# Attention and 4-bit feed-forward on one core: t for pairs of batches with its halves through DRAM, and the feed-forward as seven block products

## The reference

```python
x = x + attended(layernorm(x), ctx)      # x, ctx: (8, 256, 1024) float32
x = x + layernorm(x) @ weights + bias    # weights 1024 x 1024
# attended(text, features):
Q = text @ Wq.T + bq;  K = features @ Wk.T + bk
attn = softmax(Q @ K.T / sqrt(1024));  attended = attn @ features
# weights, from 4-bit codes of qweight, qzeros and a group index of the rows:
weights = scales[g_idx] * (where(code > 0, 1, -1) - zeros[g_idx])
```

## Time and profile before

| | |
|---|---|
| median of 3 runs (lowest, highest) | 623.54 us (623.06, 624.27) |
| the profiled execution: span | 620.2 us |
| busy: TensorE, weight loads, VectorE | 601.2, 555.8, 385.9 us |
| busy: ScalarE, GpSimd | 143.5, 125.4 us |
| matmuls | 3938 |
| moved by DMA | 60.25 MB |

### The profile page before, as it was taken

One profiled execution on the slowest core, in us unless ns is written; L12 is line 12 of the kernel. 1 busy time (PEld: TensorE's weight loads), 2 busy tenths in 40 slices (PEclk: granted clock), 3 DMA queues, 4 the chain that ended last, 5 costly groups with the idle time before them and its releaser, 6 DMA issues.

```text
span 620.2 us, 10380 instructions
## 1 busy us (share of the span) xinstructions
PE 601.2 (97%) x3938; PEld 555.8 (90%) x3938; DVE 385.9 (62%) x647; ACT 143.5 (23%) x278; POOL 125.4 (20%) x100
## 2 busy tenths in 40 slices
PE   5999999999999999999999999979999999999997
PEld 4999999999999999999999999967788888888886
DVE  5764564874865647657476674596766566567551
ACT  5321121242231322314224142154100100100100
POOL 3450000011030210301103012066132132122130
PEclk9999999999999999999999999998999999999999
DMA  8812400005042150421603306014411321221201
GB/s 275 246 35 68 165 6 2 1 1 204 2 182 89 67 204 0 161 110 46 225 0 142 129 26 246 1 35 175 166 68 70 116 85 68 106 97 68 101 35 68
DMA packets 23796, 60.25 MB, mean 97 GB/s; under 512 B 1704, under 2 KB 9904, under 8 KB 23776
## 3 DMA queue, kind: packets, MB, share of 16 engines
q1 hardware_dynamic: 23776, 59.98, 26.5%
HBM read 43.20 MB, written 16.78 MB: 97 GB/s over the span
## 4 chain that ended last, share of the span: by engine, by line
PE 90%; DVE 3%; issue 2%; DMA 2%; POOL 2%; ACT 1%; SPq 0%; ACTq 0%; POOLq 0%
PE bank L911 27%; PE bank L913 27%; PE bank L912 27%; PE bank L1005 2%; PE bank L978 2%; PE bank L1088 2%; DMA xin<-in_L_xattn_Wk 2%; POOL shared L395 1%; DVE shared L578 1%; PE bank L926 1%; DVE wrow L787 1%; PE bank L927 1%; ACT shared L433 0%; PE bank L1013 0%; ACT proj_hi L433 0%
## 5 line engine op out<-in xcount | busy, mean ns | idle before, releaser
L578 DVE TENSOR_TENSOR shared<-bank,shared 128x512 fp32r<-128x512 f32 x96 | 64.6, 687 | 139.3 <-ACT shared L433 139.3
L911 PE MATMUL bank<-shared,proj_hi 128*128 128x256 f32 x512 | 150.6, 294 | 0.0
L913 PE MATMUL bank<-shared,proj_lo 128*128 128x256 f32 x512 | 144.8, 283 | 0.0
L912 PE MATMUL bank<-shared,proj_hi 128*128 128x256 f32 x512 | 144.7, 283 | 0.0
L433 ACT ACTIVATE shared<-bank 128x512 fp32r<-128x512 f32 x96 | 56.0, 602 | 326.1 <-PE bank L1088 160.2
L911 PE MATMUL bank<-proj_hi,shared 128*128 128x512 f32 x256 | 101.7, 397 | 1.0 <-DVE proj_lo L578 1.0
L912 PE MATMUL bank<-proj_lo,shared 128*128 128x512 f32 x256 | 100.4, 392 | 0.0
L913 PE MATMUL bank<-proj_hi,shared 128*128 128x512 f32 x256 | 100.3, 392 | 0.0
L911 PEld LDWEIGHTS bank<-shared,proj_hi 128*128 128x128 f32 x512 | 98.0, 191 | 1.9
L912 PEld LDWEIGHTS bank<-shared,proj_hi 128*128 128x128 f32 x512 | 98.2, 192 | 0.4
L913 PEld LDWEIGHTS bank<-shared,proj_lo 128*128 128x128 f32 x512 | 98.0, 191 | 0.0
(11 more groups left out here) (112 smaller groups left out, 818.9 us busy)
## 6 DMA issues: line engine op xcount, KB each, us to landing
cin<-in_ctx SPq DMA_DIRECT2D x8, 1024.0 KB, 4.7
xres<-in_x SPq DMA_DIRECT2D x8, 1024.0 KB, 6.5
x_scratch<-xres SPq DMA_DIRECT2D x8, 1024.0 KB, 3.9
xin<-in_x SPq DMA_DIRECT2D x7, 1024.0 KB, 4.7
xin<-x_scratch SPq DMA_DIRECT2D x8, 512.0 KB, 3.2
cin<-x_scratch SPq DMA_DIRECT2D x8, 512.0 KB, 3.3
out<-xin SPq DMA_DIRECT2D x8, 512.0 KB, 2.6
xres<-in_L_xattn_Wq SPq DMA_DIRECT2D x7, 512.0 KB, 3.8
```

Source lines behind the costliest of these rows:

```text
L578: return dve.tensor_tensor(out_, full, hi.bitcast(F32), ALU.subtract).then_inc(done, 1)
L911: pe.matmul(out_, a_hi, b_hi, start=start, stop=False, skip_group_check=True)
L912: pe.matmul(out_, a_hi, b_lo, start=False, stop=False, skip_group_check=True)
L913: return pe.matmul(out_, a_lo, b_hi, start=False, stop=stop, skip_group_check=True)
```

## The change

**t by pairs.** The loop over batches is split in two. First all t: for four pairs of batches p, eight blocks j, 24 matmuls of 512 columns (two batches side by side) into banks 0 to 3 in turn. ScalarE and VectorE write both halves of a block into one of four staging buffers, and SyncE stores them to DRAM (256 KB each, pieces of 1 KB). The x of the next pair, its LayerNorm, `row_terms` for two batches, `pick` and `weights` (two eighths in a pair, at j = 1 and j = 4; gathers on TensorE) stand between the blocks. A finished eighth of the weights goes to DRAM too.

**Attention.** Then eight batches: scores(b) with `c_tr(b+1)` and `p_tr(b-1)` in it, then pv(b-1). tT is one buffer in four chunks; SyncE loads chunk c of t(b+1) when scores(b) has used it. Contexts have three buffers, xres two; the buffer of cn (context rows in halves) is single. In between, SyncE loads the weights (`load_w`, row tiles k and k + 4, 1 MB in one buffer); VectorE makes four sums of their quarters (`right_sums`), ScalarE and GpSimd the halves of seven blocks (`right_hi`, `right_lo`).

**Feed-forward.** For each batch, y (256 x 1024) is a 2 x 2 block matrix and so are the weights. Four sums s1 to s4 of y's blocks and four t1 to t4 of the weights' give seven products in Winograd's form (a11 b11, a12 b21, s2 t2, s1 t1, s3 t3, s4 b22, a22 t4), each 4 slices x three matmuls of 512 columns, in banks that partly go on accumulating from product to product; `added` adds each bank into the residual. a21 is copied by ScalarE, low halves of the sums are GpSimd's, of the plain blocks VectorE's. y is normalised without a stride (`ln_apply`). All loops are unrolled.

```diff
+LEFT = ("a11", "a12", "s2", "s1", "s3", "s4", "a22")
+RIGHT = ("b11", "b21", "t2", "t1", "t3", "b22", "t4")
...
+        t_stage_hi = [at(f"t_stage_hi{i}", 146.25 + 4 * i, [P, 2 * S], F32R) for i in range(4)]
...
+        cT_hi = at("cT_hi", 66, [P, NB, S], F32R)
+        cT_lo = at("cT_lo", 74, [P, NB, S], F32R)
+        tT_hi = at("tT_hi", 98.0625, [P, NB, S], F32R)
+        tT_lo = at("tT_lo", 106.0625, [P, NB, S], F32R)
+        cn_hi = at("cn_hi", 130.25, [P, QT, D], F32R)
+        cn_lo = at("cn_lo", 138.25, [P, QT, D], F32R)
...
+        w_stage = at("w_stage", 146.25, [P, 2, D], F32)
...
+        PICK = {(p, 1 + 3 * i): 2 * p + i for p in range(PAIRS) for i in range(2)}
...
+            def load_xres(b):
+                if b >= 2:
+                    sp.wait_ge(s_x1st[b % 2], 16 * (b // 2))
+                else:
+                    sp.wait_ge(s_w, 2 * NB)
+                    for n in range(2):
+                        sp.wait_ge(s_wst[n], 16 * 4)
...
+            def load_w(k):
+                if k == 0:
+                    for n in range(2):
+                        sp.wait_ge(s_ts[n], 32 * 8)
+                        sp.wait_ge(s_wst[n], 16 * 4)
+                else:
+                    sp.wait_ge(s_rlo, N_PROD * k)
+                for i in range(2):
+                    sp.dma_start(w_stage[:, i, :], w_by_tile[k + KH * i]).then_inc(s_wsl, 16)
...
+                    for dram, stage, made in ((th_dram, t_stage_hi, s_thi), (tl_dram, t_stage_lo, s_tlo)):
+                        sp.wait_ge(made, n + 1)
+                        sp.dma_start(dram[bs, :, j, :].rearrange("b p q -> p b q"),
+                                     stage[n % 4].bitcast(F32).rearrange("p (b q) -> p b q", b=2)
+                                     ).then_inc(s_ts[n % 4], 16)
...
+            load_xres(0)
+            load_xres(1)
+            load_ctx(2)
+            load_w(0)
+            for b in range(B):
+                if b + 1 < B:
+                    for c in range(3):
+                        load_t(b + 1, c)
+                if b + 2 < B and b > 0:
+                    load_ctx(b + 2)
+                if b + 1 < B:
+                    load_t(b + 1, 3)
+                if b == B - 2:
+                    sp.wait_ge(s_x1st[0], 16)
+                    sp.dma_start(yin, x1_dram[0]).then_inc(s_yl, 16)
+                if b > 0:
+                    store_x1(b - 1)
+                    if b + 1 < B:
+                        load_xres(b + 1)
+                if b in (2, 4, 6):
+                    load_w(b // 2)
...
+            made = list(R_HI)
+            for b in range(B - 1):
                 ctx_lo(b)
+                if b == B - 2:
+                    rsqrt(B)
+                if b in SPLIT:
+                    right_lo(SPLIT[b], made[:3])
+                elif b - 1 in SPLIT:
+                    right_lo(SPLIT[b - 1], made[3:])
+            right_lo(KH - 1, made[:1])
             ctx_lo(B - 1)
...
+            for name in L_LO_P:
+                left_lo(0, name)
+            add_bias(0)
+            rsqrt(B + 1)
+            for b in range(B):
+                if b + 1 < B:
+                    add_bias(b + 1)
+                    for name in L_LO_P:
+                        left_lo(b + 1, name)
+                    if b + 2 < B:
...
+            def ctx_hi(b):
+                act.wait_ge(s_cl[b % 3], 16 * (b // 3 + 1))
+                if b:
+                    act.wait_ge(s_pv, 4 * b)
+                for kt in range(QT):
+                    copy(cn_hi[:, kt, :], cin[b % 3][:, kt, :]).then_inc(s_cnhi, 1)
...
+            row_terms(0)
+            row_terms(1)
...
+            def right_sums(k):
+                dve.wait_ge(s_wsl, 32 * (k + 1))
+                (b11, b12), (b21, b22) = ([w_stage[:, i, h * HALF:(h + 1) * HALF] for h in range(2)] for i in range(2))
+                r = r_sum[k]
+                dve.tensor_tensor(r["t1"], b12, b11, ALU.subtract).then_inc(s_rsum, 1)
...
                 softmax_bias(b)
+                if b > 0:
+                    for g in range(4):
+                        residual(b - 1, g)
+                if b in SPLIT:
+                    right_sums(SPLIT[b])
+                if b == B - 2:
+                    y_stats(0)
+                    ln_apply(yin, B, s_yn)
...
+            def added(b, n):
+                dve.wait_ge(s_ff, N_PROD * b + n + 1)
+                t, h = ((0, 0), (0, 0), (0, 1), (1, 1), (1, 1), (0, 1), (1, 0))[n]
+                if n == 0:
+                    dve.wait_ge(s_rb, QT * (b + 1))
+                if n in (1, 4, 5):
+                    dve.wait_ge(s_acc, N_PROD * b + {1: 1, 4: 4, 5: 3}[n])
+                part = res[b % 3][:, t, h * HALF:(h + 1) * HALF]
+                dve.tensor_tensor(part, part, prod_bank(b, n)[:, :], ALU.add).then_inc(s_acc, 1)
...
+            for b in range(B):
+                left_lo(b, "a22")
+                if b + 1 < B:
+                    y_stats(b + 1)
+                    if b == 0:
+                        for g in range(4):
+                            residual(B - 1, g)
+                    added(b, 0)
+                    ln_apply(yin, B + b + 1, s_yn)
+                else:
+                    added(b, 0)
+                added(b, 1)
+                added(b, 2)
+                added(b, 3)
+                if b + 1 < B:
+                    left_sum(b + 1, "s1")
+                    left_sum(b + 1, "s2")
+                    left_lo(b + 1, "a11")
+                added(b, 4)
+                if b + 1 < B:
+                    left_sum(b + 1, "s3")
+                    left_lo(b + 1, "a12")
+                added(b, 5)
+                if b + 1 < B:
+                    left_sum(b + 1, "s4")
...
-            def scores(b, last=False):
-                pe.wait_ge(s_clo, NU * (b + 1))
-                s_w.wait(pe, 2 * b + 2)
...
+                        ins = three(bank[n % 4][:, :], m_hi[:, i, js], m_lo[:, i, js],
+                                    xT_hi[p % 2][:, i, :], xT_lo[p % 2][:, i, :], i == 0, i == NB - 1)
...
+            def y_tr(b, names):
+                for name in names:
+                    t, d = int(name[1]) - 1, int(name[2]) - 1
+                    pe.wait_ge(s_yn, QT * (b + 1))
...
+            def scores(b):
+                wait(pe, s_e, QT * (b - 1))
+                for j in range(NB):
+                    if j % 2 == 0:
+                        pe.wait_ge(s_clo, 4 * b + j // 2 + 1)
+                        pe.wait_ge(s_tl[j // 2], 32 * (b + 1))
+                    if b < 2 and j == 0:
+                        pe.wait_ge(s_tlo, NB * PAIRS)
                     for q in range(QT):
                         qs = slice(q * P, (q + 1) * P)
+                        ins = three(bank[b % 2][:, q * S:(q + 1) * S], tT_hi[:, j, qs], tT_lo[:, j, qs],
                                     cT_hi[:, j, :], cT_lo[:, j, :], j == 0 and q == 0, j == NB - 1)
+                    ins.then_inc(s_sc, 1)
+                    if j == 2 and b > 0:
                         p_tr(b - 1)
+                    if b + 1 < B:
+                        if j % 2 == 1:
+                            c_tr(b + 1, j // 2)
+                    elif j % 2 == 1:
+                        y_tr(0, (("a21", "a22", "a11", "a12")[j // 2],))
+            for b in range(B):
+                scores(b)
+                if b > 0:
...
+            def product(b, n):
+                if n < 2:
+                    if b >= 2 and n == 0:
+                        pe.wait_ge(s_acc, N_PROD * (b - 1))
+                    if b == 1 and n == 0:
+                        pe.wait_ge(s_lsum, 4)
+                    if b > 0 and n == 1:
+                        pe.wait_ge(s_acc, N_PROD * (b - 1) + 2)
+                elif n == 3:
...
+                fresh = n in (0, 1, 3)
+                for k in range(KH):
+                    if b == 0:
+                        pe.wait_ge(s_rlo, N_PROD * k + R_HI[RIGHT[n]] + 1)
+                    ks = slice(k * P, (k + 1) * P)
+                    ins = three(prod_bank(b, n)[:, :], l_hi[name][:, ks], l_lo[name][:, ks],
+                                r_hi[k][n], r_lo[k][n], fresh and k == 0, k == KH - 1)
+                ins.then_inc(s_ff, 1)
...
+            for b in range(B):
+                for n in range(N_PROD):
+                    product(b, n)
+                    if b == 0 and n == 1:
+                        pv(B - 1)
+                    if b + 1 < B:
+                        if n == 2:
+                            y_tr(b + 1, ("a21", "a22"))
+                        if n == 3:
+                            y_tr(b + 1, ("a11", "a12"))
...
```

1427 lines of the change are left out of this document (696 added, 731 removed).

## The result

The changed kernel takes 698.25 us (median of 4 runs, 696.83 to 698.74); the kernel before took 623.88 beside it (4 runs, 623.06 to 624.27). Ratio 1.1188, 95% interval 1.1172 to 1.1204: slower, as forecast and inside the range, 22 us above the point of 676.

The account below looks back on a forecast made before the run. TensorE's issue rate times its count was taken as the bound: 620.2 less the savings gave 580.0, new waits (a) to (g) made 672.6, and 3.3 for run medians gave 676 us, range 612 to 702.

Parts of the forecast that it names:

- The two aims: Fewer, wider matmuls: t product at 512 columns saves 10.0 us, seven feed-forward products instead of eight save 21.8 us.
- (a): Projection to t: the first t block waits for VectorE's m_lo, x_lo and copies; +3.2 us.
- (b): First pair of t: TensorE waits for onehot, 3.6 us, and weights(0,0), 4.1 us plus 1.6 of clock; +9.3 us.
- (c): From t to scores: scores(0) waits for t_lo of the last block; +1.3 us.
- (d): Attention: TensorE waits on full-queue transfers, blocked SyncE issues and late low parts; +27.6 us with clock.
- (e): First feed-forward transposes: TensorE waits for normalised y, behind statistics, GpSimd's rsqrt and contended applies; +11 us with clock.
- (f): Before the third product: GpSimd's 23.7 us chain up to the bias outlasts TensorE's 11.3 us of work; +14.6 us with clock.
- (g): Feed-forward batches: VectorE's applies take turns with GpSimd's add_bias, 3.65 us of wait in each of seven; +25.6 us.
- clock, all places: Each new wait of 3 us or more outside the feed-forward's steady part costs 1.6 us of lowered clock; 8.0 forecast.
- GpSimd did not keep pace: Answers the rival that GpSimd's 512-column subtraction takes 0.6 us or less, not 1.27: 62.7 less, 613.6 us; chance 0.16.
- The applies were held: Answers the rival that VectorE's feed-forward applies are not held, yn ready at 6.9 us: 650.4 us; chance 0.20.
- Transfers are the bound: Rival: t's 2 KB pieces move at 316 GB/s, 133 us of attention transfers in place of 102, to 707; chance 0.14.

Follow-up runs that it names:

- filler: Changed kernel plus 148 matmuls of 512 columns with unread results where TensorE stood waiting; 698.02 us, ratio 1.1211.
- packed: Changed kernel with high and low halves of t side by side, so reloads move 4096-byte pieces instead of 2048 and t's DMAs halve; 686.95 us, ratio 1.0999.
- combo: Changed kernel with bias behind the applies, ctx(2) and t(1) first, xres reload later, hand-over work moved, first pick ahead of row terms; 660.36 us, ratio 1.0601.
- best_end: combo and packed together, plus GpSimd's r_lo ahead of ctx_lo and reordered hand-over work and xres(1) load; 634.07 us, ratio 1.0163.

## Why the forecast was right, and where it was 22 us low

**Sign and size.** The two aims hold: without idle time and without the clock's share, TensorE took 620.2 - 19.0 - 1.6 = 599.6 us before and 695.6 - 95.6 - 28.7 = 571.3 after, 28.3 less where 31.8 were forecast. Idle time and clock together, 124 us against 21 before, outweigh them. The total of the waits was nearly right, 84.6 us forecast without clock, 80.3 measured, but by errors that cancel:

| | forecast, without clock | measured |
|---|---|---|
| (a) projection to t | 3.2 | 2.6 |
| (b) first pair | 7.7 | 5.4 |
| (c) t to scores | 1.3 | 1.2 |
| (d) attention | 24.4 | 33.2 |
| (e) first y transposes | 9.4 | 11.6 |
| (f) before the third product | 13.0 | 11.0 |
| (g) forecast in seven batches, found in six | 25.6 | 15.3 |
| clock, all places | 8.0 | about 29 |

**The step that failed is the clock**: "I add this 1.6 once to each new wait of 3 us or more". The earlier trace rows shows one wait of 3.0 us in a kernel that is otherwise dense; and the forecast left the rule out at two of its own waits, the 3.6 of (b) and the 3.8 on ctx(7). In the changed kernel waits follow each other every few us, the windows of attention and hand-over stand at 0.87 and 0.81, and the term is 28.7, not 8.0. The span was missed by 695.6 - 672.6 = 23.0: 20.7 of clock and 3.5 of the aims, less 4.3 of waits in the places of the table, and 3.1 of idle time in others: the waits at the start, taken over at 8.6 us, are now 11.8. The run filler shows that the waits cause the clock. It shows as well that inside the attention this is bookkeeping: had the clock stayed up there, TensorE would have waited longer. By the forecast's own terms the stretch from the first scores to the first product makes about 140 us (102 of work, 33.8 of waits in (d) and (e), 4.8 of clock), and it took 159.7. What was forecast too short there is the transfers' time, next.

**The aims** gave 3.5 us less than forecast. The forecast took 0.227 us from start to start at 512 columns; in the changed kernel it is 0.232 in the t stage (30 steps from 279.75 to 286.71) and 0.231 in the feed-forward (26 steps from 620.77 to 626.77), at a granted clock of 1.00 in the first window. Over 1440 such matmuls that is some 6 us. Why they stand further apart is not shown.

**(d)** had the right kind of cause, and the wrong rate and blocker. The 41.9 MB at 412 GB/s were 102 us; the busy engines moved 347 GB/s, at which they are 121. The 412 came from rows of 4096-byte pieces; packed shows that t in 2048-byte pieces, with twice the issues, costs 11.3 us more than in pieces of 4096. The walk let load_w block the queue; it waited 2.4 us, load_xres 42.9. The forecast had seen that wait ("load_xres waits until store_x1 has landed (3.9 us)") and priced it at an empty queue's landing; with the queues full it was up to 11.1 us. **(e)** had another link: the forecast let the statistics of y(0) follow residual(5) at once and GpSimd's ctx_lo(6) end last; the load of y(0) landed later, 4.97 us of wait on VectorE, and 9.4 became 11.6. **(f)**: the chain on GpSimd was as described, 23.3 us from the start of ctx_lo(7) to the end of the bias where 22.6 were counted; part of its wait was taken earlier, 3.6 us on r_lo. **(g)**: turns as forecast, in six batches of seven, and the wait shorter (2.55 against 3.65): from rsqrt to the last apply it took 6.4 us, not 7.2. A batch takes 23.8 us, not 24.5. **(b)**: onehot 3.3 against 3.6; wt 2.1 against 4.1, and clock for both.

**Rivals.** GpSimd did not keep pace (1.29 us a subtraction; its 613.6 should read 613.3, 676 less 62.7). The applies were held. *Transfers are the bound* was the nearest miss: 19 of its 31 us of excess (121 against 102), true of the attention, though not of the sum. **Luck.** That the total of the waits came out within 5 us is luck: (d) was 9 us too short, (g) 10 too long.

## What to carry to other kernels

A detour through DRAM has to be priced by the pieces and the number of transfers in which it moves, and together with the waits of the one queue that issues it: here a "load after store has landed" cost up to 11.1 us with the queues full, where 3.9 were counted. Where blockers may stand in a row, read the queue's waits again after each repair and remove them together, or the test says nothing. Where waits come every few microseconds, take the clock from the whole stretch, not one loss per wait. And some 30 us saved on a saturated engine are no gain if the order that they need leaves it idle for 95.6 us: the old loop with everything inside it had 19.0.

## What was not expected of the hardware

- Filling idle stretches with 148 matmuls of no use left the time as it was (698.02 against 698.25) and raised the clock from 0.944 to 0.980.
- With the reloads of t in pieces of 4096 instead of 2048 bytes, and half as many of them, the busy engines moved 372 instead of 347 GB/s between 340 and 440 us; but with 2048-byte pieces the same quotient was 360 in combo. From the issue of the first chunk of t to that of the context, six issues later, SyncE's queue took up to 4.1 us with the queues full.
- The four sums of the weights' quarters on VectorE (512 columns, two SBUF operands) took 0.68 us for the first one, which ended as GpSimd's ctx_lo began, and 1.66, 1.76 and 1.75 on average for the other three, beside it. In best_end, where ctx_lo(7) runs from 442.71 to 448.68, it is the other way round: 1.77 and 1.67 for the first two, 0.68 for the last two, from 449.15 on.
